# The second normalization's chain and the first one's statistics change places in an attention-and-router kernel

## The reference, cut to what matters

```python
# layernorm over the 2048 columns of each row
h = layernorm(x)
q = Wq @ h + bq;  k = Wk @ ctx + bk;  v = Wv @ ctx + bv      # 256 x 2048 each, 8 heads of 32
# windowed attention: column t sees the 16 columns from t-8 to t+7
dots[h, t, w] = (q[h, :, t] . k[h, :, t + w - 8]) / sqrt(32)
att = softmax(dots) applied to v
x1 = x + tanh(g_xattn) * (Wo @ att + bo)
# the second normalization, again over the columns, and a router over 64 experts
y = layernorm(x1)
scores = softmax(y @ Wr^T + rbias)                  # one row of 64 for each of the 256 rows
keep the 8 largest; w_sum = their sum; mix = kept weights @ expert_bias
out = x1 + tanh(g_ffn) * (y * w_sum + mix)
```

## Time and profile before

| | |
|---|---|
| median of 3 runs | 1546.06 us (1544.34 to 1550.62) |
| the profiled execution's own time | 1549.06 us |
| its span, first to last instruction | 1547.0 us |
| TensorE matmul busy | 1457.9 us, 94% of the span |
| VectorE busy | 1232.8 us, 80% |
| ScalarE busy | 1156.2 us, 75% |
| GpSimd busy | 1160.6 us, 75% |
| DMA | 49.1% of 16 engines' span in the main queue |
| mean granted TensorE clock | 0.974 of full speed |

### The profile page before, as it was taken

How to read it: one execution, slowest core, us unless ns; L and a number is a source line. 1 busy time by engine, 2 the same in 40 slices (tenths; PEclk the granted TensorE clock), 3 DMA queues, 4 the chain that set the end, 5 groups by cost and what they waited for, 6 DMA issues and landing times.

```text
span 1547.0 us, 66674 instructions
## 1 busy us (share of the span) xinstructions
PE 1457.9 (94%) x28162; PEld 1196.4 (77%) x28162; DVE 1232.8 (80%) x2938; ACT 1156.2 (75%) x2025; POOL 1160.6 (75%) x1126
## 2 busy tenths in 40 slices
PE   4799999999999999999999999999999999999986
PEld 3577877878887888888788888878888887778764
DVE  5477887878888787888888788888878888787774
ACT  3588877778787877888787787878778787767652
POOL 4587777788777878778787887878788787677661
PEclk9799999999999999999999999999999999999896
DMA  7454455554545555454555545455554545434232
GB/s 231 122 127 107 127 149 140 145 161 113 162 131 140 144 154 162 112 161 133 140 144 154 162 114 162 131 140 147 152 161 114 160 133 140 123 82 134 57 77 90
DMA packets 365576, 210.39 MB, mean 136 GB/s; under 512 B 294496, under 2 KB 295520, under 8 KB 361056
## 3 DMA queue, kind: packets, MB, share of 16 engines
q1 hardware_dynamic: 365280, 206.14, 49.1%
HBM read 136.88 MB, written 33.55 MB: 110 GB/s over the span
## 4 chain that ended last, share of the span: by engine, by line
PE 60%; DVE 19%; issue 6%; ACT 6%; POOL 5%; DMA 2%; SPq 1%; POOLq 0%; ACTq 0%; DVEq 0%
PE ps_j L1123 26%; PE ps_s L1183 9%; PE ps_a L1148 7%; PE ps_r L1225 6%; PE ps_s L1123 5%; DVE prob_t L908 4%; DVE st_x L915 2%; PE ps_s L1178 2%; POOL prob L495 2%; PE ps_a L1202 2%; PE ps_t L1165 1%; PE ps_a L1203 1%; DMA x_in<-x_dram 1%; DVE st_in L820 1%; DVE nt_x L814 1%
## 5 line engine op out<-in xcount | busy, mean ns | idle before, releaser
L488 POOL TENSOR_TENSOR score<-score,p_inv 128x384 f32<-128x384 f32 x256 | 219.2, 856 | 110.5 <-DVE p_inv L902 107.6
L495 POOL TENSOR_TENSOR prob<-score,prob 128x384 f16<-128x384 f32 x256 | 262.6, 1026 | 32.8 <-ACT prob L660 31.6
L1183 PEld LDWEIGHTS ps_s<-kv_win,q_col 32*32 32x32 f32 x16384 | 197.2, 106 | 59.2 <-issue 58.7
L1183 PE MATMUL ps_s<-kv_win,q_col 32*32 32x48 f32 x16384 | 233.8, 205 | 4.0 <-issue 3.8
L908 DVE STREAM_TRANSPOSE prob_t<-prob 128x512 f32<-128x512 f32 x256 | 177.1, 701 | 68.0 <-POOL prob L495 67.4
L469 POOL TENSOR_TENSOR c_lo<-c_in,c_hi 128x1024 fp32r<-128x1024 f32 x64 | 152.7, 2385 | 91.0 <-ACT c_hi L634 91.0
L1148 PEld LDWEIGHTS ps_a<-prob_t,v_diag 128*128 128x128 f16 x6528 | 175.8, 98 | 51.0 <-DVE prob_t L908 34.0
L1148 PE MATMUL ps_a<-prob_t,v_diag 128*128 128x48 f16 (+2 forms) x6528 | 188.3, 183 | 26.9 <-DVE prob_t L908 20.2
L464 POOL TENSOR_TENSOR att_lo<-att,att_hi 128x512 fp32r<-128x512 f32 x128 | 161.7, 1275 | 50.1 <-ACT att_hi L620 48.8
L598 ACT ACTIVATE kv_win<-ps_j,v_bias 128x512 f16<-128x512 f32 x128 | 108.2, 847 | 104.0 <-PE ps_j L1123 104.0
L1123 PE MATMUL ps_j<-c_hi,wkv_hi 128*128 128x512 f32 x512 | 172.5, 419 | 14.1 <-POOL c_lo L469 7.0
(11 more groups left out here) (149 smaller groups left out, 3320.0 us busy)
## 6 DMA issues: line engine op xcount, KB each, us to landing
v_diag<-v_turn SPq DMA_DIRECT2D x512, 68.0 KB
c_in<-ctx_dram SPq DMA_DIRECT2D x64, 512.0 KB, 4.9
x_in<-x_dram SPq DMA_DIRECT2D x64, 512.0 KB, 5.7
x_res<-x_dram SPq DMA_DIRECT2D x64, 512.0 KB, 4.7
out_dram<-x SPq DMA_DIRECT2D x32, 1024.0 KB, 8.0
c_sq<-ctx_dram SPq DMA_DIRECT2D x60, 512.0 KB, 5.6
x<-ctx_dram SPq DMA_DIRECT2D x4, 512.0 KB, 7.0
x<-experts_dram SPq DMA_DIRECT2D x2, 512.0 KB, 10.2
```

Source lines behind the costliest of these rows:

```text
L488: pool.tensor_tensor(score[:, u], score[:, u], p_inv[:, u, :].unsqueeze(2).to_broadcast([P, HALF, KEYS]), ALU.mult).then_inc(pm_rdy, 1)
L495: pool.tensor_tensor(part(prob[:, u % 2], 1)[:, :, 0:KEYS], score[:, u], part(prob[:, u % 2], 0)[:, :, 0:KEYS], ALU.subtract).then_inc(pl_ ...
L1183: ins = pe.matmul(s[head(h), n * KEYS:(n + 1) * KEYS], q_col[head(h), g, at:at + SUB], kv_win[c % 2][head(h), 0, g, at:at + KEYS], start=F ...
```

## The change

`inverse_root` is cut in two, `root_seed` (the four operations that give the seed) and `root_steps` (any of the three rounds). `ln1`, the first normalization's chain, calls both in a row as before. The second normalization's chain leaves the end of step c == 0: its aggregation and seed now open step c == 1, its first round stands between turn(2) and turn(3), the other two rounds behind turn(3). In those same steps the two `stats_in` leave the place before largest(0): the first now stands behind shift(0), the second behind shift(1). No operation is added or dropped. The new order holds in the steps c == 1 of the sequences b = 1 to 15 (for b = 15 there are no input statistics left; for b = 16, the drain, no turns, so that the order is the old one).

```diff
-            def inverse_root(chain, base, mv, var, half, nt, rs, neg_mean, ready):
+            def root_seed(chain, base, mv, var, half, rs, neg_mean):
 ...
                 dve.wait_ge(chain, base + 3)
                 dve.tensor_scalar(rs[:].bitcast(I32), var[:].bitcast(I32), -0.5, float(RSQRT_SEED),
                                   ALU.mult, ALU.add).then_inc(chain, 1)
-                for i in range(3):
+
+            def root_steps(chain, base, half, nt, rs, ready, steps):
+
+                for i in steps:
                     dve.wait_ge(chain, base + 4 + 3 * i)
 ...
+                if routing:
+
+                    need(dve, st2_rdy, b * (NCH * G))
+                    dve.memset(pad[:, 2:3], 0.0).then_inc(aggr2, 1)
+                    for g in range(G):
+                        dve.bn_aggr(mv_x1[:, g], st_x1[:, g]).then_inc(aggr2, 1)
+                    need(dve, aggr2, b * (G + 1))
+                    root_seed(root2, (b - 1) * ROOT, mv_x1, var_x1, half_x1, rs_x1, neg_mean_x1)
                 if before:
                     turn(2, -1)
+                if routing:
+                    root_steps(root2, (b - 1) * ROOT, half_x1, nt_x1, rs_x1, ln2_rdy, range(1))
+                if before:
                     turn(3, -1)
-                if stats:
-
-                    ch, db = place(c, 4)
+                if routing:
+                    root_steps(root2, (b - 1) * ROOT, half_x1, nt_x1, rs_x1, ln2_rdy, range(1, 3))
+                if stats and not routing:
+
                     need(dve, x_ld[ch], (b + db + 1) * 16)
                     stats_in(1, ch)
                     stats_in(0, ch)
 ...
                     shift(0)
+                if stats and routing:
+                    need(dve, x_ld[ch], (b + db + 1) * 16)
+                    stats_in(1, ch)
 ...
                     shift(1)
                 if finishing(b, c):
                     finish(0)
+                if stats and routing:
+                    stats_in(0, ch)
                 if now:
                     largest(2)
 ...
-                if c == 0 and seq(b - 1):
-
-                    need(dve, st2_rdy, b * (NCH * G))
-                    dve.memset(pad[:, 2:3], 0.0).then_inc(aggr2, 1)
-                    for g in range(G):
-                        dve.bn_aggr(mv_x1[:, g], st_x1[:, g]).then_inc(aggr2, 1)
-                    need(dve, aggr2, b * (G + 1))
-                    inverse_root(root2, (b - 1) * ROOT, mv_x1, var_x1, half_x1, nt_x1, rs_x1, neg_mean_x1, ln2_rdy)
```

More of the change, by code:

```diff
@@ L831, in ln1 @@
                 need(dve, aggr1, (b + 1) * (G + 1))
-                inverse_root(root1, b * ROOT, mv_in, var_in, half_in, nt_in, rs_in, neg_mean_in, ln1_rdy)
+                root_seed(root1, b * ROOT, mv_in, var_in, half_in, rs_in, neg_mean_in)
+                root_steps(root1, b * ROOT, half_in, nt_in, rs_in, ln1_rdy, range(3))
             dve.wait_ge(wkh_rdy, 1)
@@ L933, in step @@
                 routing = c == 1 and seq(b - 1)
+                if stats:
+                    ch, db = place(c, 4)
+                if routing:
[5 more added lines that the diff above has]
+                    root_seed(root2, (b - 1) * ROOT, mv_x1, var_x1, half_x1, rs_x1, neg_mean_x1)
                 if before:
                     turn(2, -1)
+                if routing:
+                    root_steps(root2, (b - 1) * ROOT, half_x1, nt_x1, rs_x1, ln2_rdy, range(1))
+                if before:
                     turn(3, -1)
-                if stats:
-                    ch, db = place(c, 4)
+                if routing:
+                    root_steps(root2, (b - 1) * ROOT, half_x1, nt_x1, rs_x1, ln2_rdy, range(1, 3))
+                if stats and not routing:
                     need(dve, x_ld[ch], (b + db + 1) * 16)
```

## The result

The changed kernel takes 1585.17 us (median of 4 runs, 1580.9 to 1587.74), the kernel before beside it 1548.34 us (4 runs, 1544.34 to 1553.49): a ratio of 1.0233, 95% interval 1.0192 to 1.0274. Two later comparisons gave 1.0223 (1.0187 to 1.0259) and 1.0232 (1.0215 to 1.0249). The profiled execution took 1587.74 us, its span is 1585.6 us, 38.6 us above the span before.

The account below looks back on a forecast made before the run. TensorE was taken to bound most stretches, VectorE step c == 1; +40 + 6 - 7 = +39 us on the profiled 1549.06 gave 1588, less 3.0 for the runs' median 1585 us. Range of 8 in 10: 1551 to 1612.

Parts of the forecast that it names:

- Bound at both ends of step c == 1: Step c == 1 is the one stretch where VectorE bounds both ends; what it gains or loses there goes to the end.
- The first round and the turns: Start of step c == 1: one operation waits for low(3), turn(3) comes earlier, TensorE's gap goes, 0.40 us gained.
- The last two rounds: three held: Behind turn(3), three of six operations wait for GpSimd, until 712.72, 713.97 and 715.2: 4.2 us of VectorE's time added.
- The rival with two held: Behind turn(3), two operations caught, not three: 3.0 us added, 1.9 us for a sequence, 1564 us; chance 0.20.
- scores(2): TensorE's scores(2) waits for shift(0) and starts at 717.4: a gap of 2.3 us, 1.9 us behind the old time.
- The input statistics: 1.25 us leave the place before largest(0); behind shift(0) and shift(1), with the earlier TensorE, they fill VectorE's idle 1.10 us.
- 13 x 3.1 us: In 13 sequences turn(3) ends 3.1 us later over the step, and attend(1) of the next with it: 40 us.
- Clock, +6 us: TensorE's granted clock falls behind the new gap in half of the sequences, 0.7 to 1 us each; bounds 0 and 52.
- Sequences 14 and 15, -7 us: TensorE's gaps of 3.67 and 2.43 us go there: -7 us for both sequences, bounds 0 and -16.
- The rival "faster": Nothing is caught behind turn(3), TensorE's gaps at the first boundary go: -22, 1524 us; chance 0.10.

Follow-up runs that it names:

- the first experiment: Kernel before, with only the input statistics of steps c == 1 moved behind shift(0) and shift(1): 1552.53 us, ratio 1.003.
- The kernel with nothing held: Changed kernel in its order, the rounds' two small tiles in PSUM, so each operation has at most one SBUF input: 1535.65 us, ratio 0.9914.
- the version with the statistics back: Changed kernel's chain order, the rounds' two small tiles in PSUM, input statistics back ahead of largest(0): 1532.35 us, ratio 0.9881 to the kernel before.
- one tile in PSUM: Changed kernel's order, with only half of the rounds' two tiles in PSUM and nt in SBUF: 1561.28 us, ratio 1.0094.
- the chain alone: Changed kernel with the input statistics back ahead of largest(0), only the chain split and moved: 1610.8 us, ratio 1.0413.

## Why the prediction was right, point by point

Predicted were 1585 us, measured 1585.17. The agreement to the microsecond is luck in part: the sequences 1 to 13 got 48.6 us longer where I had 46, and 14 and 15 got 9.8 us shorter where I had 7, and the two cancelled. By its own steps:

**Bound at both ends of step c == 1.** Right. The holding of VectorE in this step comes out again as the length of the sequence, hardly reduced: taking it away took 3.1% off the changed kernel.

**The first round and the turns.** Right. turn(3) was to start at 709.19, which is 732.08 with the offset; it starts at 732.07. The gap of 0.40 us went, and L817 was held by low(3) as L814 was before, 0.96 us.

**The last two rounds: three held.** Right to 0.1 us. The ends were given as 712.72, 713.97 and about 715.2, which is 735.61, 736.86 and 738.09; measured are 735.60, 736.83 and 738.05. The rival with two held went by a margin of 0.09 us. The margin held in 12 of the 13 sequences; in the third it didn't, and that sequence shows the rival's gap (1.07 us, given as 1.1). The rule of the Trainium skill (SBUF — State Buffer, "Who interferes with whom") that a VectorE instruction with two SBUF inputs and a GpSimd instruction that reads SBUF exclude each other is borne out here, and so is its reverse: with one of the inputs in PSUM the same operation passes at 0.16 us beside context_low.

**scores(2).** Right: the gap given as 2.3 us is 2.28, and the start at 717.4 (740.29) is 740.30. It was to stand there 13 times, and stands there 12.

**The input statistics.** The step is wrong as I put it, and right only in the company of the rest. I had them fill 0.59 us of VectorE's wait for exponent(0). On the kernel before they fill nothing, since ScalarE and then TensorE's scores(1) hold VectorE up to the old time (rows of the first experiment), and cost 4.6 us. In the changed kernel ScalarE has idled by then (exponent(0) starts at 740.27 after 3.60 us of waiting for shift(0)), VectorE has no idle time marked from 729 to 742 us, and taking 1.25 us out of the way to shift(0) is worth some 25 us in all. Of the 1.10 us of idle time 0.65 went; the wait of 0.33 us for ScalarE's half of the values is one of 0.45 us now (750.83). I had summed them as if the wait that they fill were the old one. It came out right since the delay of shift(0) was large.

**13 x 3.1 us.** The term is sound: the shortest middle sequences are 93.0 us against 90.0, and attend(1) of the next boundary is 3.41 us late in sequence 7. I expected a gap of 0.6 us on TensorE there. None is marked in sequence 7, as the slower clock behind 740 us had made TensorE late by itself. In 3, 8 and 11, where the clock stayed at 1.00, TensorE waits 0.26 to 0.30 us before attend(0) and 0.33 to 0.34 us before attend(1) at that boundary, 0.6 us together.

**Clock, +6 us.** Right in size, but not as I had it put together. I took a fall in half of the sequences at 0.7 to 1 us. In the profiled run the clock falls behind the new gap in 10 of the 13, in eight for the short time (about 0.5 us each by the figures above) and in two, 6 and 13, for the long one (about 1.7): some 7 us, an estimate from these means. Sequences 1 to 13 are 48.6 us longer, 8.3 more than 13 x 3.1. What else is in the 8 us is another gap in the fifth sequence (6.5 us over before), which the kernel before has 0.37 us shorter, with a granted clock of 0.50 from 594 to 600 us behind it:

```profile
592.70 0.78 PE L1163 MATMUL ps_a<-prob_t,v_diag 128*128 128x48 f16 x25 [1.38 <-issue]
```

I had no term for that. Sequence 1 has a second fall at its end (4.6 us over before), and sequence 3 with its two held operations takes off 1.

**Sequences 14 and 15, -7 us.** Right in sign, short in size: -9.8. TensorE's timeline, sequence 14 and 15:

```profile
1390.63 1.43 PE L1163 MATMUL ps_a<-prob_t,v_diag 128*128 128x32 f16 x51 [1.60 <-DVE prob_t L912]
...
1490.09 0.34 PE L1193 MATMUL ps_s<-mask,ident_b 128*128 128x384 bf16 x1 [1.06 <-DVE score L897]
```

I had both gaps before attend(1) vanish. In 15 the one of 2.43 us did; in 14 it shrank from 3.67 to 1.60 us, since the first round's last operation in its new place is held for 2.36 us by context_low (1387.60) ahead of turn(3), just as the chain was before. In the two other profiles of the changed kernel it isn't, and that gap is gone in 14, too.

**The rival "faster".** The kernel with nothing held shows what it would have given: 1536 us, not 1524. Of the 12 us between, 3 are no error of the working: the kernel before had a median of 1549.19 us beside this run, and I had counted from 1546.06. Sequences 1 to 13 got 1.7 us shorter in sum, where I had 5.6; the missing 4 us are the statistics again (with them back it is 5.6). Sequences 14 and 15 got 12.7 us shorter, where I had up to 16. Two things that I had left out stand in the rows, without a price for each: turn(3), free of the chain, waits for low(3) (0.64 us at 707.28 in the version with the statistics back), and the gap at the next boundary of sequence 14, 2.20 us in the kernel before, is there in every version (2.20 us at 1360.18, 2.50 in this one).

## What to carry to other kernels

Before small VectorE operations are moved, read what GpSimd runs at the new place: one of 0.16 us on two inputs in SBUF costs whatever is left of the GpSimd operation that was there first, and a dependent chain pays for each of GpSimd's operations in a row. Giving one input of each to PSUM removed that price altogether, and was worth more (-1.3%) than any order tried. And two parts of one change must not be priced against the same old profile: a move that loses by itself can win behind a wait that the other part creates.

## What the runs showed that I had not expected

- 0.02 us decide. In one sequence of the changed kernel the operation that was to be held began 0.02 us before context_low and passed, and the sequence was 0.7 us shorter than the next shortest (92.4 against 93.1).
- How often the clock falls goes with the length of TensorE's gap before scores(2): behind 0.7 to 1.1 us (one tile in PSUM) in none of 13 sequences, behind 2.1 to 2.5 us in 30 of 38, behind 3.5 us (the chain alone) in all 13, and there for the long time in 12. Gaps of one and the same length go both ways.
- Stalls of TensorE that the profile can't attribute ("issue", up to 1.92 us) grew when 9 matmuls a sequence were added, and stand in the sequences that are 2 to 5 us longer than the undisturbed ones. An experiment that adds instructions isn't neutral here, and a filler has to be read by its undisturbed sequences alone.
